# A linear-memory attention layer and its routed experts on one core: the state update of the last chunk is left out, and the steps have a new order

## The reference

```python
for c0 in range(0, S, 128):                     # 4 chunks
    g = grad of sum((silu(k @ W1.T) @ W2.T - v) ** 2) by (W1, W2), per token,
        at the W of the chunk's start, times 0.1, its norm cut to 1
    for each token of the chunk:
        Sm = eta * Sm - theta * g
        Wm = (1 - alpha) * Wm + Sm              # Wm at every token is kept
    h = silu(q @ W1(token).T); out(token) = h @ W2(token).T
```

## Time and profile before

| | |
|---|---|
| median of 3 runs | 583.77 us (579.64, 583.77, 592.17) |
| the profiled execution: span from the first to the last instruction | 546.5 us |
| its granted TensorE clock, mean | 0.947 of 2.4 GHz |
| busy shares of the span | TensorE 84%, DVE 71%, ACT 62%, POOL 61% |
| memory traffic | 44.20 MB read, 19.22 MB written |

### The profile page before, as it was taken

The page is one execution under the profiler, slowest core; times in us unless marked ns, Lnnn a source line. Parts: engine busy times, 40 slices in busy tenths (PEclk is TensorE's granted clock), DMA queues, the critical chain, the costliest instruction groups (busy, mean ns, idle before and its releaser), DMA issues.

```text
span 546.5 us, 11654 instructions
## 1 busy us (share of the span) xinstructions
PE 461.7 (84%) x3702; PEld 358.3 (66%) x3702; DVE 385.6 (71%) x1125; ACT 339.1 (62%) x834; POOL 332.0 (61%) x457
## 2 busy tenths in 40 slices
PE   4678989999988998989989999888788578775993
PEld 2356757867857675767858786656667466564883
DVE  3356984978689887696897986979576446543562
ACT  1357556786776665767676768674457356742673
POOL 2005165265495846789677797567337776666677
PEclk9798899999999999999998999999779798987898
DMA  8324424643536273536656354557754647346652
GB/s 216 103 81 115 119 59 108 157 105 92 146 99 179 57 189 76 155 69 156 170 101 170 79 162 113 130 126 232 166 136 107 183 140 207 116 155 212 193 150 69
DMA packets 64140, 73.76 MB, mean 135 GB/s; under 512 B 20078, under 2 KB 50991, under 8 KB 64081
## 3 DMA queue, kind: packets, MB, share of 16 engines
q1 hardware_dynamic: 53408, 46.65, 31.6%
q0 software_dynamic: 8848, 25.44, 18.0%
q10 hardware_dynamic: 1824, 0.93, 0.7%
HBM read 44.20 MB, written 19.22 MB: 116 GB/s over the span
## 4 chain that ended last, share of the span: by engine, by line
PE 34%; DVE 22%; POOL 13%; ACT 12%; issue 9%; DMA 6%; SPq 3%; POOLq 0%; ACTq 0%; DVEq 0%
PE bank L1225 8%; DVE kq_in L543 7%; POOL sorted_rows L1010 5%; PE bank L589 4%; PE bank L502 4%; ACT rows L943 3%; PE bank L520 3%; PE bank L1202 2%; DVE grad_w L794 2%; DVE y L914 2%; DMA hq<-hq 2%; DMA front<-in_hidden_t 2%; DMA sorted_rows<-rows,index 2%; PE bank L950 2%; POOL rstd L935 2%
## 5 line engine op out<-in xcount | busy, mean ns | idle before, releaser
L1264 POOL DMA_INDIRECT out<-os,xs_token x71 | 70.2, 988 | 32.1 <-issue 12.6
L1010 POOL DMA_INDIRECT sorted_rows<-rows,index x64 | 69.7, 1089 | 30.0 <-POOL index L1006 13.7
L543 DVE SCALAR_TENSOR_TENSOR kq_in<-shared,conv_w,kq_in 128x256 f32<-128x256 f32 x144 | 70.1, 545 | 11.7 <-ACT kq_in L537 11.6
L1225 PE MATMUL bank<-shared,front 128*128 x280 | 74.4, 413 | 2.0 <-issue 1.9
L502 PE MATMUL bank<-front 128*64 128x256 f32 x512 | 63.2, 398 | 13.9 <-DMA bias_t<-in_bias_t 7.5
L589 PE MATMUL bank<-front 128*128 128x256 f32 x256 | 62.2, 390 | 1.7 <-DVE kq L670 1.7
L1225 PEld LDWEIGHTS bank<-shared,front 128*128 128x128 f32 x280 | 55.3, 208 | 11.2 <-issue 3.7
L502 PEld LDWEIGHTS bank<-front 128*64 128x64 f32 x512 | 36.1, 142 | 34.6 <-DMA bias_t<-in_bias_t 7.5
L589 PEld LDWEIGHTS bank<-front 128*128 128x128 f32 x256 | 47.6, 194 | 9.2 <-DVE kq L670 2.1
L1259 ACT ACTIVATE os<-bank,rs 128x256 f32<-128x256 f32 x70 | 35.7, 560 | 19.0 <-DVE rs L1248 17.2
L914 DVE SCALAR_TENSOR_TENSOR y<-bank,rms,gt 128x256 f32<-128x256 f32 x64 | 26.5, 476 | 26.8 <-POOL rms L910 12.5
(11 more groups left out here) (211 smaller groups left out, 1249.3 us busy)
## 6 DMA issues: line engine op xcount, KB each, us to landing
front<-sorted_rows SPq DMA_DIRECT2D x71, 130.0 KB
front<-in_hidden_t SPq DMA_DIRECT2D x16, 512.0 KB, 5.0
decay<-gate_clear SPq DMA_DIRECT2D x16, 512.0 KB, 4.1
y<-in_hidden POOLq DMA_DIRECT2D x16, 512.0 KB, 5.6
q<-kq_in SPq DMA_DIRECT2D x64, 64.0 KB
carry<-carry_rows SPq DMA_DIRECT2D x32, 128.0 KB
hq<-hq SPq DMA_DIRECT2D x64, 64.0 KB
w<-state SPq DMA_DIRECT2D x32, 64.0 KB, 2.8
```

What stands on the lines that cost most here:

```text
L543: dve.scalar_tensor_tensor(dst, raw[g][:, kind, :, tap:tap + P], conv_w[:, kind, tap:tap + 1], dst, ALU.mult, ALU.add))
L1010: pool.indirect_dma_start(sorted_rows[:, :], bass.IndirectOffsetOnAxis(index[i2][:, b:b + 1], 0), R[:, b, :], None, bounds_check=NE * REGI ...
L1225: ins = pe.matmul(both[:, i, :], xs_t[t % TURNED][:, i, k, :], w_expert[:, k, bass.ds(expert, 1), :], start=k == 0, stop=k == KH - 1)
L1264: pool.indirect_dma_start(out[:, :], bass.IndirectOffsetOnAxis(xs_token[t % LOADS][:, i:i + 1], 0), os_[o][:, i, :], None, bounds_check=TO ...
```

## The change

In the last chunk (pieces c to f) nothing reads the state that upd makes. `updates(c)` is false there, and these steps are left out: the keep_rows and ends transfers, end_c, g_dec, ck, ch, upd, the copies of the state and of w2_t, the transfers into W12, and the two transposes. Waits for them are left out too (`of_update` names the last update there is, `until` counts the transfers that are left). The ring of `retrieve` counts 4 uses per piece there instead of 6, so its two banks are free for the experts after the last `out`. The copy of k and v on ACT also waits for `sq_h` of two pieces before. And `ORDER` is another one throughout, from its third step on.

```diff
--- before.py
+++ after.py
@@ -437,7 +437,7 @@
 
     pro = Slots("pro", banks[0:3], NC * G * 9)
     lrn = Slots("lrn", banks[3:4], NC * G * 5)
-    rtv = Slots("rtv", [both[:, i, :] for i in range(2)], NC * G * 6)
+    rtv = Slots("rtv", [both[:, i, :] for i in range(2)], NC * G * 4 + (NC - 1) * G * 2)
     epi = Slots("epi", banks[4:6], NC * G * 6 + len(TABLES))
     late = LateSlots((pro, lrn, rtv, epi))
 
@@ -453,6 +453,21 @@
     def arrived(c, g, transfers):
 
         return (c * (G // 2) + g // 2 + 1) * 16 * transfers
+
+    def updates(c):
+
+        return c < NC - 1
+
+    def of_update(c, g, name):
+
+        n = c * G + g - 2
+        return f"{name}.{n}" if n < (NC - 1) * G else f"{name}.-1"
+
+    def until(c, g, transfers, last):
+
+        if updates(c):
+            return arrived(c, g, transfers)
+        return arrived(NC - 2, G - 1, transfers) + (g // 2 + 1) * 16 * last
 
     def load_next(c, g):
 
@@ -623,7 +638,7 @@
             for j in range(2):
                 ins = pe.transpose(bank[:, (2 * kind + j) * P:(2 * kind + j + 1) * P], of[:, j, :], ident[:, :])
         mark("pe", n("kv_n_ps"), ins)
-        wait("act", n("kv_n_ps"), o2("ck"), o2("e2"))
+        wait("act", n("kv_n_ps"), of_update(c, g, "ck"), o2("e2"), o2("sq_h"))
         flat_n = kv_n[i2][:, :, :, :].rearrange("p i b d -> p i (b d)")
         act.activation(flat_n[:, 0], bank[:, 0:2 * P], ACT.Copy)
         mark("act", n("kv_n"), act.activation(flat_n[:, 1], bank[:, 2 * P:4 * P], ACT.Copy, scale=2.0))
@@ -642,18 +657,20 @@
         C, E_ = (flat(resp[i2][:, w]) for w in range(2))
         dec_a, dec_e = (flat(decay[i2][:, w]) for w in range(2))
 
-        wait("sp", n("carry_t"), o2("ab_q"), o2("g_dec"))
+        wait("sp", n("carry_t"), o2("ab_q"), of_update(c, g, "g_dec"))
         sp.dma_start(carry_rows[i2].rearrange("w b t -> (w b) t"), carry_t[i2][:, :]).then_inc(s_short[i2], 16)
-        sp.dma_start(keep_rows[i2].unsqueeze(1), keep_t[i2][NB:2 * NB, P - 1:P], allow_slow_non_contiguous=True).then_inc(s_short[i2], 16)
-        sp.wait_ge(s_short[i2], arrived(c, g, 2))
+        if updates(c):
+            sp.dma_start(keep_rows[i2].unsqueeze(1), keep_t[i2][NB:2 * NB, P - 1:P], allow_slow_non_contiguous=True).then_inc(s_short[i2], 16)
+        sp.wait_ge(s_short[i2], until(c, g, 2, 1))
         wait("sp", o2("ab_h"))
         for w, side in enumerate((slice(0, D), slice(D, P))):
             row = carry_rows[i2, w].rearrange("b t -> (b t)").unsqueeze(0)
             sp.dma_start(flat(carry[i2][side, :, :]), spread(row, 0, D)).then_inc(s_carry[i2], 16)
-        sp.dma_start(ends[i2][:, 1, :], spread(keep_rows[i2].unsqueeze(0), 0, P)).then_inc(s_carry[i2], 16)
+        if updates(c):
+            sp.dma_start(ends[i2][:, 1, :], spread(keep_rows[i2].unsqueeze(0), 0, P)).then_inc(s_carry[i2], 16)
         yield
         dve.wait_ge(s_dec[i2], arrived(c, g, 1))
-        wait("dve", o2("ck"), o2("ch"))
+        wait("dve", of_update(c, g, "ck"), of_update(c, g, "ch"))
         mark("dve", n("scan_e"), dve.tensor_tensor_scan(E_, dec_e, flat(ident_nb[:, :, :]), 0.0, ALU.mult, ALU.add))
         yield
         wait("dve", n("scan_e"), o2("p2"))
@@ -674,15 +691,18 @@
         yield
         who, wide_e = wide_engine(c, g)
         wide_e.wait_ge(s_q2[i2], arrived(c, g, 4))
-        wide_e.wait_ge(s_carry[i2], arrived(c, g, 3))
+        wide_e.wait_ge(s_carry[i2], until(c, g, 3, 2))
         wait(who, o2("zq_ps"))
         mark(who, n("ab_q"), wide_e.tensor_tensor(ab_q[i2][:, :, :], q2[i2][:, :, :], carry[i2][:, :, :], ALU.mult))
-        pool.wait_ge(s_carry[i2], arrived(c, g, 3))
+        if not updates(c):
+            yield
+            return
+        pool.wait_ge(s_carry[i2], until(c, g, 3, 2))
         wait("pool", o2("g_dec"))
         mark("pool", n("end_c"), pool.tensor_scalar(ends[i2][:, 0, :], carry[i2][:, :, P - 1], 1.0, None, ALU.mult))
         yield
 
-        dve.wait_ge(s_carry[i2], arrived(c, g, 3))
+        dve.wait_ge(s_carry[i2], until(c, g, 3, 2))
         wait("dve", n("end_c"), o2("upd_ps"))
         mark("dve", n("g_dec"), dve.tensor_tensor(g_dec[i2][:, :, :, :], spread(ident_g[:, :, :].unsqueeze(1), 1, NB),
                                                   spread(ends[i2].rearrange("p w b -> p b w").unsqueeze(3), 3, D), ALU.mult))
@@ -712,7 +732,7 @@
         mark("pe", n("z_ps"), ins)
         wait("act", n("z_ps"), o("d_silu"))
         mark("act", n("t_z"), act.activation(wide(t_z[:, :, :]), z, ACT.Tanh, scale=0.5))
-        wait("dve", n("t_z"), o("ch"), o("h_ps"), o("sq_h"))
+        wait("dve", n("t_z"), of_update(c, g + 1, "ch"), o("h_ps"), o("sq_h"))
         mark("dve", n("h"), dve.scalar_tensor_tensor(wide(h[:, :, :]), wide(t_z[:, :, :]), 1.0, z, ALU.add, ALU.mult))
         lrn.freed_by(i, n("h"))
         yield
@@ -783,13 +803,14 @@
         mark("pool", n("inv_g"), pool.tensor_tensor(small[:, 4, :], small[:, 3, :], minus_half[:, 0:NB], ALU.pow))
 
         yield
-        who, wide_e = wide_engine(c, g)
-        wait(who, n("h"), o2("upd_ps"), n("scan_c"))
-        mark(who, n("ch"), wide_e.tensor_tensor(ch[i2][:, :, :, :], spread(h[:, :, :].unsqueeze(2), 2, 2), at_end(i2), ALU.mult))
-        yield
+        if updates(c):
+            who, wide_e = wide_engine(c, g)
+            wait(who, n("h"), o2("upd_ps"), n("scan_c"))
+            mark(who, n("ch"), wide_e.tensor_tensor(ch[i2][:, :, :, :], spread(h[:, :, :].unsqueeze(2), 2, 2), at_end(i2), ALU.mult))
+            yield
         wait("pool", n("inv_g"), n("theta0"), o("grad_w"))
         mark("pool", n("weight"), pool.tensor_tensor(small[:, 5, :], small[:, 4, :], theta[i2][:, :], ALU.mult))
-        wait("dve", n("weight"), o2("upd_ps"), o2("out_ps"), o2("zq_ps"))
+        wait("dve", n("weight"), of_update(c, g, "upd_ps"), o2("out_ps"), o2("zq_ps"))
         wgt = small[:, 5, :].unsqueeze(2)
         mark("dve", n("grad_w"), dve.tensor_tensor(grad_w[i2][:, :, :, :], grad[:, :, :, :], spread(spread(wgt, 2, D).unsqueeze(1), 1, 2), ALU.mult))
         yield
@@ -1285,23 +1308,23 @@
 ORDER = (
-    "p0p0p0p1p0p0p1p0p0p0p0p0p0p0p2l0p1p1p1p1p1p1s0p1l0l0l0s0l0p1p1l0l0l0s0s1s1p3s0p1l0l1p2p2p2s0l0s1p4p2p2s0p2p2l1l1r0l1p2p2"
-    "p2s0r0l1p2s1l1r0s2s2l1l1l1s1s2l2p3p3p3l1s2l2p3p3s1l2p3r0p3r1e0e0s2l2e0s1p3l2p3p3p5l2p7r0l2s3l2r1l2s3p3l3r1l2p4p4p4p4s2l3"
...
-    "x0x0x0x0x0x0x0x0x0x0x0x0x0x0x0x0x0x0x0x0x0x0x0x0x0x0x0x0x0x0x0x0x0x0rex0x0x0rdx0x0x0rex0x0"
+    "p0p0p1p0p0p0p0p0p0p0p0p0l0p0p1p1p1p1p1s0p1p1l0s0l0l0p1l0s0l0l0p1l0p1s0s0l0p2l1s1l0p1s0l1s1s1s1p2s0p2p2r0p2p3p2l1p2p2p2l1"
+    "p2r0p2p2r0l1l1l1r0l1l1s2l2e0r0s1s2l2p3s1s2e0l1l2e0p3p3l2p3p3p3e0p3p7l2e0p3r0s2p3p3r1e0s1s2p3l2l2s2l2r1s3p4s3e0r1e0l2l3e0"
...
+    "x0x0x0x0x0x0x0x0x0x0x0x0x0x0x0x0x0x0x0x0x0x0x0x0x0x0x0x0x0"
 )
```

More of the change, by code:

```diff
@@ new lines @@
+    "e3r4l5p7p7s5e3s5p7l5e3p7p7p7e3r4l5p7e1e2e1l5e1l6p7e2p7s6e2e1p7s6l6r4pbe1l6e2l6p7l6e2e3r3e2s6e4s6s7e4l6l6r5l6p8e3l6s6e4e2"
+    "p8p8p8e4p8l7r5p8r5p8e3p8l7p8p8l7l6l7s7e2r4pcp8e3e2r5e4s7r6e3e3s6s7r5l7e5s7l7l7e5e4l7e3p9l7p9e5r6e3p9r6p9p9l8p9e5p9e4p9e4"
+    "l7e3s8r5l8p9s7e4e3e4p9s8l8pae4l8r6p9s8l8e6e3e5s8s8r6s7e6l8r7e4pae5l8e6l8pal8r7e4par7pal9papapas9e5par7e5l9r6l8e6e4e5e4s9"
+    "s8l9l9e5s9papae5s9l9e6r7e5e7s8s9pal9l9r8e6l9e5l9e7pbe7r8pbpbr8pblapbpbpbpbe6r7e7pbpbe6l9lasae6s9lae6sae5lae6s9e5r8r9e6la"
```

24 lines of the change are left out of this document (10 added, 14 removed).

## The result

The changed kernel takes 590.75 us in the median of 4 runs (588.53 to 594.9), the kernel before 583.54 us (579.64 to 592.17) on the same chip: a ratio of 1.0174, with an interval from 1.0116 to 1.0233. It is slower; the forecast was 1.6% faster, and the range ended at 587. Of a kernel's runs the ratios leave out those over 1.5% above its fastest; medians and ranges take in all.

The account below looks back on a forecast made before the run. From the last chunk's emptying, POOL's sends were taken as the bound, their start hanging on SP's queue. Gains 8 + 4.2 + 0.3 less 2.3 and 1 gave 9.2 us: span 537.3 plus 37.3 is 574.6 us, range 562 to 587.

Parts of the forecast that it names:

- the last of the rivals: Chunks 0 to 2: new order worse or better than the old by 4 us; only widens, no chance given.
- The start of the experts: SP's queue before the experts' first load: hq ahead of the wait, ends and W12 gone; 8 of 10.3 us taken.
- a first send no earlier than 409: Sign of being wrong: POOL's first send that late means the SP queue was not what held it; forecast near 403.5.
- Removed work: Last chunk's update steps: TensorE at most 4 us before the first load, POOL 0.3 us, the rest hidden.
- The wait put down to keep_rows: SP's 5.5 us wait before the first load: given nothing, as carry_rows remains; bounds 0 and 5.5 us.
- The end of the last epilogue: Before table 2's tiles: pad positions known earlier, TensorE's 6.42 us stall goes; worth 4.2 us, bounds 0 and 6.4.
- The pads, forecast before 478 us: Sign of being right: SP's wait at the pads gone and the pad transfers issued before 478 us.
- What is added: Added costs: 2.3 us on POOL, 1 us for the hq stop; ACT's sq_h wait 0, at most 16 x 0.30.
- The stop for the hq of piece f: SP stops between the loads of pairs 4 and 5, TensorE runs dry: 0 to 3.5 us, 1 taken.
- The slower rival: Pads ahead of pairs 22 and 23, zq of piece f missing grad_w: 597 us, chance 0.12.
- What lies around the span: Median run less profiled span, 583.8 - 546.5 = 37.3 us, taken to stay.
- the better rival: Experts: POOL's other 8 us of idleness go too, through two more PSUM banks: 567, with keep_rows 563; chance 0.22.

Follow-up runs that it names:

- the run for TensorE's part: Old order without the removed steps, TensorE again doing the last chunk's update matmuls, results unread: 574.11 us, ratio 0.9826 to the kernel before, on a 580 chip.
- the first run of the old order: Changed kernel's code with the old ORDER, the removed steps left out, nothing else moved: 533.6 us, ratio 0.9777 to the kernel before, on a 547 chip.

## Why the prediction was wrong

**The step that failed** is the last of the rivals: "the new order of chunks 0 to 2 is worse or better than the old by 4 us: TensorE's idle share there is small, so this only widens". It had no chance of its own and stood in the sum at nothing. It measured 21.7 us at the first load on one chip (410.8 to 389.0 us). The reason given was the mistake: a small idle share does not bound what an order can cost. TensorE was 90% busy between 30 and 400 us in both orders and had done 92 matmuls fewer in the worse one; its busy time also holds the slower clock. What the runs showed in its place are the four sends in POOL's queue, with others' small operations behind them: without them the two orders took the same time. I counted where steps of the last chunk and the experts stand, and not one inversion of the thousands in the chunks before.

**The start of the experts** was forecast 8 us earlier and came 13 to 15 us later, with the first send at 428.1 us; the prediction named a first send no earlier than 409 as a sign that it was wrong, since then SP's queue was not what held it. What the step says of SP's queue is right, hq in front of the carry step, W12 and ends gone. But a queue that is reordered for an earlier start helps only if its inputs come as before, and they came later.

**Removed work** was mis-sized, in the good direction: 4 upstream, 1.9 for ends and W12, 0.3 behind. With the old order the first load comes 8.5 us earlier on one chip (397.6 to 389.0), and the stretch from POOL's first send to its end shrinks there from 133.3 to 129.2 us. The whole is 12 us against 6. That the upds beside POOL's stream "give nothing by themselves" was wrong by up to 4.1 us; which engine gives them stays open, since the run for TensorE's part was too coarse.

**The wait put down to keep_rows** was given nothing, and that was right. Without keep_rows SP still stands from 377.06 to 382.11 us in the first run of the old order, 5.05 us for 5.5 of the earlier trace rows, behind carry_rows alone. The rule of the Trainium skill's page DMA: Bandwidth & Descriptors, Anatomy of one DMA, about 2 us whatever the size, gave the same answer, though that section describes transfers that POOL starts and this one is SP's. The trace agrees that the wait stays, and not with the size: 5.05 us here, and in that run three other carry steps waited 0.95, 1.09 and 3.00 us.

**The end of the last epilogue** came as forecast on the 547 chip: no wait of TensorE for sorted rows over 2 us is left in the second half of the experts, where the earlier trace rows has 6.42 us and the old order without the removed steps 8.14 us. SP's wait at the pads fell from 7.1 to 3.0 us. POOL's stream is 127.5 us (428.12 to 555.6) against 129.1 in that old order (401.60 to 530.7), 1.6 us shorter, where 4.2 for the stall less 2.3 for the added work makes 1.9. The pads, forecast before 478 us, came at 492.7, but 82.0 us behind the first load, not 92.4. On the 580 chip the stall did not go: SP took 21.24 us to start the eight pad transfers, and TensorE stood 13.03 us. The old order with two buffers for y, on such a chip, took 14.59 us and stood 12.30 us, so this stall comes with the kind of chip and not with the order.

**What is added:** ACT's wait for sq_h is in every run of the old order too, and these are faster than before: nothing, as said. The stop for the hq of piece f cost TensorE nothing visible; there is no wait for a load beside it in the new order on the 547 chip.

**The slower rival** had a chance of 0.12 for another mechanism, pads and zq of piece f, which did not happen on the 547 chip. A rival with the right mechanism, the steps of one queue in the wrong places for the others, stood there with 4 us. **What lies around the span** was taken for 37.3 us; it is 1 to 2, the rest was the difference of two chips. This cost the forecast nothing, since a gain in per cent comes out nearly the same. The 563 of the better rival should be 562 (574.6 - 8 + 1 - 5.5); nothing hangs on it.

## What to carry to other kernels

Where one order sets the queues of several engines, its change is a change of every stage, also of those whose code is the same: look for steps that changed places in each stage (how to price them no run here shows), and let the busy share of the first engine be no bound on it. Look in the queue of the engine with the longest single steps (here four scatters, 5 us) for the small operations behind them that others wait for; the sum of all waits for that engine told these two orders apart where the busy shares did not, but it did not rank every run. And split such a change before it is kept: the removal with the old order is 2.2% faster than before and 4.3% faster than the changed kernel, the best version of all that ran.

## What the runs showed of the hardware

One program took 6 to 7% longer on some chips: medians of before from 544.8 to 547.4 us on three chips, 579.5 to 583.5 in three sessions on others. The ratios of the two orders agree on both kinds (1.022 and 1.0174), but the time is not lost evenly. The changed kernel has its first load at 410.8 us on a 547 chip and at 416.1 us on a 580 chip, and from there to the end 145.9 and 171.2 us; the old order has 389.0 and 391.5 us, then 145.4 and 174.6 us (the later ones with two buffers for y). So nearly all of the difference lies in the experts' stage. One part of it is the pads: SP starts the eight transfers in 8.5 to 9.6 us in every profile from a 547 chip and in 14.6 to 21.2 us in every one from a 580 chip.

Four indirect transfers of POOL, one after the other, held its queue for 5.1 us (333.48 to 338.57 us). TensorE's clock gave back little: with 8.4 us of lost clock recovered (15.9 to 7.5), the first load came 3.3 us earlier, on another chip that is itself 2.4 us faster to this place in the old order.
